# Projection-weight casts over two steps, a home for the weight of each quarter, and large roundings taken apart, in a gated cross-attention kernel

## The reference, cut to what matters

```python
ln_out = _ln(hidden_states, ln_w, ln_b)
q  = _fp8_linear_pertensor(ln_out, wq, ...)      # 16 heads; k, v: 8 groups; qx: 16 heads
core = _gqa(_ln(q), _ln(k), v)                   # self attention
xout = _gqa(_ln(qx), _ln(kx), vx)                # kx, vx = cond @ w_kv_x
cat  = concatenate([core, xout])
catq = _div_clamp_fp8(cat, proj_smooth)          # clip, then round to 8-bit floats
return einsum(catq, wproj) * (proj_in_scale * proj_w_scale)
```

## Time and profile before

| what | before |
|---|---|
| runs | 1636.44 us median of three (1634.56 to 1636.97) |
| the profiled execution, its own time | 1630.85 us |
| its span | 1629.1 us |
| TensorE busy | 1574.2 us, 97% of the span |
| VectorE busy | 1150.1 us, 71% |
| ScalarE busy | 1015.2 us, 62% |
| GpSimd busy | 486.0 us, 30% |
| DMA | 196.62 MB, 121 GB/s in the mean |
| granted TensorE clock | 0.995 in the mean |

### The profile page before, as it was taken

The page is one execution under the profiler, slowest core; times in us unless marked ns, Lnnn a source line. Parts: engine busy times, 40 slices in busy tenths (PEclk is TensorE's granted clock), DMA queues, the critical chain, the costliest instruction groups (busy, mean ns, idle before and its releaser), DMA issues.

```text
span 1629.1 us, 27708 instructions
## 1 busy us (share of the span) xinstructions
PE 1574.2 (97%) x9392; PEld 1221.4 (75%) x9392; DVE 1150.1 (71%) x2380; ACT 1015.2 (62%) x2855; POOL 486.0 (30%) x515
## 2 busy tenths in 40 slices
PE   7989979999998999999999999999999999999998
PEld 6878766666777767777777777777777777777887
DVE  6358865444997778888888887677777777898322
ACT  4354335553467877877878777777777777875100
POOL 1000222223524333443333443433443343420000
PEclk9999989999999999999999999999999999999999
DMA  8030648885663232364243353121152121110011
GB/s 304 27 109 28 229 167 271 274 270 175 215 228 124 75 135 79 101 237 143 81 136 99 106 199 116 46 77 58 46 201 66 46 109 58 46 39 7 22 38 39
DMA packets 75813, 196.62 MB, mean 121 GB/s; under 512 B 6896, under 2 KB 27376, under 8 KB 69168
## 3 DMA queue, kind: packets, MB, share of 16 engines
q1 hardware_dynamic: 70016, 176.50, 31.6%
q0 software_dynamic: 5680, 18.62, 3.9%
HBM read 147.12 MB, written 47.97 MB: 120 GB/s over the span
## 4 chain that ended last, share of the span: by engine, by line
PE 71%; DVE 8%; ACT 5%; DMA 1%; issue 1%; POOL 1%; SPq 0%; POOLq 0%; ACTq 0%; DVEq 0%
PE bank L2518 9%; PE bank L2517 9%; PE bank L99 8%; PE bank L101 8%; PE bank L100 8%; PE bank L2579 6%; PE bank L2603 5%; PE bank L2568 4%; PE bank L1423 4%; PE bank L1443 4%; PE bank L2589 3%; ACT t_sc L2734 2%; POOL t_rs L2482 1%; PE bank L1403 1%; DVE x_res L1782 1%
## 5 line engine op out<-in xcount | busy, mean ns | idle before, releaser
L2517 PE MATMUL bank<-t_half,t_xh 128*128 128x256 f16 (+1 forms) x1024 | 309.3, 326 | 0.7 <-DVE t_hn L2839 0.7
L2518 PE MATMUL bank<-t_half,t_xh 128*128 128x256 f16 (+1 forms) x1024 | 306.0, 326 | 0.0
L2479 POOL TENSOR_SCALAR t_ve<-t_ss 128x4 f32<-128x4 f32 (+1 forms) x128 | 25.6, 200 | 580.0 <-DVE t_ss L2835 554.4
L2734 ACT ACTIVATE t_sc<-bank,t_mx 128x128 f32<-128x128 f32 x512 | 180.1, 386 | 17.7 <-DVE t_mx L2875 13.1
L2839 DVE TENSOR_TENSOR t_hn<-bank,t_rs 128x256 f32<-128x256 f32 (+1 forms) x256 | 130.0, 549 | 63.4 <-POOL t_rs L2482 63.4
L2482 POOL TENSOR_TENSOR t_rs<-t_ve,t_mhalf 128x4 f32<-128x4 f32 (+1 forms) x128 | 171.0, 1336 | 10.7
L2517 PEld LDWEIGHTS bank<-t_half,t_xh 128*128 128x128 f16 x1024 | 100.3, 98 | 66.7 <-issue 1.4
L2518 PEld LDWEIGHTS bank<-t_half,t_xh 128*128 128x128 f16 x1024 | 100.2, 98 | 66.0
L2772 ACT ACTIVATE t_y<-bank,smooth 128x128 bf16<-128x128 f32 x512 | 139.3, 401 | 2.3 <-DVE t_cq L1303 2.3
L2603 PE MATMUL bank<-t_wp,t_cq 128*128 128x512 f16 x512 | 130.7, 379 | 0.0
L2579 PE MATMUL bank<-t_hT 128*128 128x128 f32 x1024 | 126.2, 276 | 2.7 <-ACT t_hT L2761 2.3
(11 more groups left out here) (355 smaller groups left out, 3878.7 us busy)
## 6 DMA issues: line engine op xcount, KB each, us to landing
t_xh<-xq_scratch SPq DMA_DIRECT2D x64, 512.0 KB, 3.5
t_cr<-in_ctxT_dram SPq DMA_DIRECT2D x64, 256.0 KB, 2.7
t_half<-w_half SPq DMA_DIRECT2D x12, 1024.0 KB, 7.6
y_rows<-s_y SPq DMA_DIRECT2D x39, 256.0 KB, 2.4
e_w<-in_w_units_dram SPq DMA_DIRECT2D x8, 1024.0 KB, 11.8
w_rows<-in_w_qkv_dram SPq DMA_DIRECT2D x8, 1024.0 KB, 5.6
xq_scratch<-z_xs SPq DMA_DIRECT2D x16, 512.0 KB, 3.3
t_slot<-w_plain SPq DMA_DIRECT2D x4, 2048.0 KB, 8.4
```

What stands on the lines that cost most here:

```text
L2517: nc.tensor.matmul(out, rows[:, k, kind, :], w[0][:, k, a:b], start=k == 0, stop=False)
L2518: last = nc.tensor.matmul(out, rows[:, k, kind, :], w[1][:, k, a:b], start=False, stop=k == KT - 1)
L2734: last = nc.scalar.activation(sc[:, h, :], b3[4 + part][:, n, :], ACT.Exp, bias=mx[:, h:h + 1], accum_out=sm[:, h:h + 1])
```

## The change

Four things are done. The projection weight gets four buffers, one for each quarter, each in the upper 8 KB of the slot that holds the quarter's q weight; one array of the dense stage (`xT_lo1`) moves to where the single buffer was, and the wait for `pj_ps` goes. The four casts of a quarter stand in two steps, 16 q + 1 and 16 q + 2, in each one before the second square of the keys and one behind the head copies. The large roundings are taken apart: in steps 4 to 7 the clamp stands behind the maxima and the two operations on the bits behind the first half of the item's rounding, in front of `normalise_b`. The slices are grouped anew over steps 1 to 6, from step 3 on with two of them in front of the second square. `LATE_FIRST` goes from 8 to 9. Cut out of the diff below are only lines that hand `m` and `quarter` on to the output product.

```diff
-LATE_FIRST = 8
+LATE_FIRST = 9
...
+    def clamp(self, dve, n):
+        y = self.y[n % 2]
+        dve.wait_ge(self.y_in, n * 4 + 4)
+        self.nc.vector.tensor_scalar(y[:].bitcast(F16), y[:], F16MAX, -F16MAX, ALU.min, ALU.max
+                                     ).then_inc(self.clamped, 1)
+
     def rounded(self, dve, c, k):
+        self.clamp(dve, c * KT + k)
+        self.rounded_bits(dve, c * KT + k)
+
+    def rounded_bits(self, dve, n):
...
+        bits = self.y[n % 2][:].bitcast(I16)
         dve.wait_ge(self.clamped, n + 1)
...
-        self.hi, self.lo = ([at(f"xT_{n}{c}", kb + 8 * i, [P, KT, CW], F32R) for c, kb in enumerate((kvx, wq, wqx, 64))]
-                            for i, n in enumerate(("hi", "lo")))
+        self.hi = [at(f"xT_hi{c}", kb, [P, KT, CW], F32R) for c, kb in enumerate((kvx, wq, wqx, 64))]
+        self.lo = [at(f"xT_lo{c}", kb, [P, KT, CW], F32R) for c, kb in enumerate((kvx + 8, 122, wqx + 8, 72))]
...
-    wp = sb("wp", 122, [P, 8, D], F16)
...
-    LAST_ROWS = (1, 3, 4, 5)
-    ROW_PIECES = {1: range(0, 3), 2: range(3, 4), 3: range(4, 6), 4: range(6, 9), 5: range(9, 12), 6: range(12, 16)}
+    wp = [sb(f"wp{q}", SLOTS[homes[q][WQ_]] + 8, [P, 8, D], F16) for q in range(Q)]
+    LAST_ROWS = (4, 5, 6, 7)
+    ROW_PIECES = {1: (0,), 2: (1, 2), 3: (3, 4, 5), 4: (6, 7, 8), 5: (9, 10, 11, 12), 6: (13, 14, 15)}
...
-            if i - 1 in LAST_ROWS:
-                sh.store(sp, (C - 1) * KT + LAST_ROWS.index(i - 1))
+            if i in LAST_ROWS:
+                sh.store(sp, (C - 1) * KT + LAST_ROWS.index(i))
...
-                last = nc.tensor.matmul(bank[5][:], cq[par][:, h, :], wp[:, h, :], start=h == 0, stop=h == KH - 1)
+                last = nc.tensor.matmul(bank[5][:], cq[par][:, h, :], wp[quarter_of(m, quarter)][:, h, :], start=h == 0,
+                                        stop=h == KH - 1)
...
         def wproj(quarter, part):
             i, a = divmod(part, 2)
-            if quarter and part == 0:
-                act.wait_ge(pj_ps, quarter * B)
             if part == 0:
                 act.wait_ge(wraw_in, quarter * 16 + 16)
...
-        def rows_part(i, part):
-            pieces = ROW_PIECES.get(number(i), ())
-            if part < len(pieces):
-                k, v = divmod(pieces[part], 4)
+        def rows_parts(i, first, last):
+            for piece in ROW_PIECES.get(number(i), ())[first:last]:
+                k, v = divmod(piece, 4)
                 sh.scaled(act, C - 1, k, (v,))
 
         def wproj_part(i, part):
-            if isinstance(i, int) and i % B == 2 and i < M:
-                wproj(i // B, part)
+            if isinstance(i, int) and i % B in (1, 2) and i < M:
+                wproj(i // B, 2 * (i % B - 1) + part)
...
                 if part:
-                    rows_part(m - 1, 0)
+                    wproj_part(m - 1, 0)
+                    rows_parts(m - 1, 0, 1 if number(m - 1) < FIRST else 2)
                 act.wait_ge(a_ps, m * 2 + part + 1)
...
             if has(i):
                 heads_out(i)
-            rows_part(i, 1)
-            wproj_part(i, 0)
+            wproj_part(i, 1)
+            if number(i) >= FIRST:
+                rows_parts(i, 2, 3)
             if has(i + 1):
                 values(i + 1, 1 - par)
-            rows_part(i, 2)
-            wproj_part(i, 1)
-            rows_part(i, 3)
-            wproj_part(i, 2)
+            rows_parts(i, 1 if number(i) < FIRST else 3, 4)
             if has(i - 1):
                 scaled_out(i - 1, quarter)
-            wproj_part(i, 3)
...
             if has(i - 1):
                 maxima(i - 1)
+                if number(i) in LAST_ROWS:
+                    sh.clamp(dve, (C - 1) * KT + LAST_ROWS.index(i))
...
             if has(i - 2):
                 rounded(i - 2, par, 0)
+            if number(i) in LAST_ROWS:
+                sh.rounded_bits(dve, (C - 1) * KT + LAST_ROWS.index(i))
...
-            if number(i) - 1 in LAST_ROWS:
-                sh.rounded(dve, C - 1, LAST_ROWS.index(i - 1))
```

More of the change, by code:

```diff
@@ L2599, in attend, with output_heads @@
                 last.then_inc(pv_ps, 1)
-        def output_heads(par, heads):
+        def output_heads(m, par, quarter, heads):
             for h in heads:
-                last = nc.tensor.matmul(bank[5][:], cq[par][:, h, :], wp[:, h, :], start=h == 0, stop=h == KH - 1)
+                last = nc.tensor.matmul(bank[5][:], cq[par][:, h, :], wp[quarter_of(m, quarter)][:, h, :], start=h == 0,
+                                        stop=h == KH - 1)
             return last
@@ L2612, in output_begin, with output_end @@
                 pe.wait_ge(x_in, m)
-            output_heads(par, range(QH))
-        def output_end(m, par):
-            output_heads(par, range(QH, KH)).then_inc(pj_ps, 1)
+            output_heads(m, par, quarter, range(QH))
+        def output_end(m, par, quarter):
+            output_heads(m, par, quarter, range(QH, KH)).then_inc(pj_ps, 1)
         def output(m, par, read, quarter):
             output_begin(m, par, read, quarter)
-            output_end(m, par)
+            output_end(m, par, quarter)
         def step(i, par, quarter):
@@ L2632, in step @@
             if has(i - 3):
-                output_end(i - 3, 1 - par)
+                output_end(i - 3, 1 - par, quarter)
             if has(i - 1):
@@ L2679, in wproj @@
             raw = slots32[homes[quarter][SPARE]]
-            last = nc.scalar.activation(wp[:, 4 * i + 2 * a:4 * i + 2 * a + 2, :], raw[:, i, 2 * a:2 * a + 2, :], ACT.Copy)
+            last = nc.scalar.activation(wp[quarter][:, 4 * i + 2 * a:4 * i + 2 * a + 2, :], raw[:, i, 2 * a:2 * a + 2, :],
+                                        ACT.Copy)
             if a:
                 last.then_inc(wp_in, 1)
-        def rows_part(i, part):
-            pieces = ROW_PIECES.get(number(i), ())
-            if part < len(pieces):
-                k, v = divmod(pieces[part], 4)
+        def rows_parts(i, first, last):
+            for piece in ROW_PIECES.get(number(i), ())[first:last]:
+                k, v = divmod(piece, 4)
                 sh.scaled(act, C - 1, k, (v,))
         def wproj_part(i, part):
-            if isinstance(i, int) and i % B == 2 and i < M:
-                wproj(i // B, part)
+            if isinstance(i, int) and i % B in (1, 2) and i < M:
+                wproj(i // B, 2 * (i % B - 1) + part)
         def squares_a(m):
```

5 lines of the change are left out of this document (removed).

## The result

The changed kernel takes 1617.31 us in the median of four executions (1614.39 to 1620.32), the kernel before 1636.7 (1634.56 to 1637.09): a ratio of 0.9884, interval 0.9864 to 0.9905. It is faster by 19 us, as forecast in sign, and by more than forecast: 1621.8 was the time, 1619.0 the lower end of the range.

The account below looks back on a forecast made before the run. TensorE's nine waits for VectorE's normalisation, 13.8 us, were taken as the recoverable loss. Savings over steps 2 to 51 summed to 14.7 us, taken as 14.6: 1636.44 - 14.6 = 1621.8 us, range 1619.0 to 1627.0.

Parts of the forecast that it names:

- the limit of 5.76 us: Latest start of VectorE's normalisation (L2839) after a step's start without cost; anything later is paid one for one.
- home per quarter: Separate projection-weight buffers remove the first cast's wait for the last old-weight product; costed at nothing, 8 us of load cover.
- late weights: LATE_FIRST 9 moves a late chunk's high parts off step 18; step 19 loses its 0.7 us more than step 35.
- The two operations beside the power: Bits operations on VectorE during GpSimd's power, steps 4 to 7: cost between 0.0 and 1.0 us per step, 0 to 0.1 taken.
- The near row: Head-stage pairing of power and two VectorE operations: at most 0.4 us longer power, 0.3 covered, 0 to 0.1 per step.
- that rival: Steps 4 to 7: bits operations start only after GpSimd's power, 4.5 us lost where 0.2 counted; 1626.1 us, chance 0.12.
- The rival of the window that is not free: ScalarE cast pushes the keys' second square; steps 3, 19, 35, 51 keep about 1 us each; 1625.8 us, chance 0.13.
- the rival of late raw weights: Casts in steps 1, 17, 33, 49 wait for 2 MB loads; 1641 us if each lands 17 us later, chance 0.02.
- the cover and the slack: 8 us between the raw weight's landing and step 1's cast, and 0.4 us by which the normalisation may be late.

Follow-up runs that it names:

- 14 stalls, two operations: Changed kernel plus two unread 128x1024 ScalarE operations in front of the output rows in 14 steps (8, 10, ..., 34): 1635.36 us, ratio 1.0001.
- three stalls put back: Changed kernel plus three unread 128x1024 ScalarE operations in front of the output rows in steps 18, 34 and 50 alone: 1628.59 us, ratio 0.9951.
- The two kernels with 14 long stalls: Changed kernel plus three or four unread ScalarE operations in front of the output rows in 14 steps: 1661.4 us with three, 1674.81 with four.

## Why the prediction was wrong in its time, point by point

**What bounds the kernel, and the limit of 5.76 us.** Right. There were nine stalls in front of one instruction, and every one that was forecast to go went, but for the 0.3 us of step 3 and the 0.2 of step 6. Step 6, with L2842 at 5.94, is 0.18 beyond the limit and 0.2 too long.

**Casts over two steps, home per quarter, late weights, roundings, slices.** Steps 35 and 51 gave 2.26 and 2.27 (2.23 forecast for each), step 19 2.89 (2.96), steps 5 and 7 1.70 and 1.96 (1.66, 1.93), step 6 1.49 (1.47), step 3 1.93 (1.80), step 2 0.43 (0.4). The sum is 14.9 us where 14.7 was worked out, and 15.0 in the stretch. The runs with one part alone bear out the parts of it, 7.1 for the casts and 4.4 for the roundings with the late chunk; the rest, 3.5, is there only together. About 2.6 of it is in steps 2 and 3, which need the slices and the rounding out of the way as well as the casts, and 0.9 in steps 5 and 7, where slices had stood in front of the output rows.

**The two operations beside the power.** The near row was the right one: 0.12 us longer power (up to 0.4 allowed), operations of 0.69 us. By the lock that the Trainium skill describes ("SBUF — State Buffer", "SBUF: two separate sides") they would, as operations in a two-port mode, have had to wait for the end of the power; in this pairing the trace does not agree (the one of 557.95 took 0.69 us inside a power that ran from 557.65 to 559.41), and that rival is out. The rival of the window that is not free is out as well (step 1's square starts on time). The raw weights were there. One price in the rival of late raw weights was reckoned wrong: with 17 us more at each of four loads, 8.6 beyond the cover and the slack, the time would be 1621.8 + 34.4 = 1656 us and not 1641; nothing else hangs on it.

**The step that failed** is the one from the profiled execution to the median: "The median of the three runs is 5.6 above the profiled one; the change touches nothing of that difference". It touches a good part of it, about 4 us by the changed kernel's own runs. Behind a stall with 1.74 us of idle time or more TensorE's clock falls to half, in some executions, and costs 1.6 us each time. The kernel before has four such stalls (steps 3, 19, 35, 51). Its profiled execution happened to have none of the falls, so its trace showed stalls at their bare price. The changed kernel has no such stall left. Of the 4.5 us by which 1621.8 missed 1617.3, 0.4 is a stretch that shrank by 15.0 instead of 14.6, and the rest is this step.

How much that is: medians give 1636.1 (74 executions of the kernel before in this study) less 1617.4 (eight of the changed one), 18.7 us; the stretch gives 15.0; 3.7 us are left, 2 to 3 falls in an ordinary execution. The intervals are wide: 15.5 to 22.3 us for the first comparison and 16.0 to 23.9 for the second, so 15.0 lies only just outside of both. The part in front of step 1 does not explain the rest, for it was not shorter in the changed kernel (505.51 and 509.45 us against 504.96, 505.76 and 506.61). All the kernels together say more. For each, this is how much less its median is than that of the kernel before on the same chip, how much less its stretch is than 905.78 with its own falls taken out, and what the median has beyond the stretch:

| kernel | median less by | stretch less by | left |
|---|---|---|---|
| changed, again | 18.7 | 15.0 | 3.7 |
| no slice in front of the output rows | 18.5 | 15.6 | 2.9 |
| casts alone | 9.9 | 7.1 | 2.7 |
| LATE_FIRST 8 again | 16.5 | 14.7 | 1.8 |
| 14 stalls, two operations | -0.9 | -2.5 | 1.7 |
| slices in their old places | 14.2 | 13.0 | 1.3 |
| roundings alone (four long stalls) | 3.9 | 4.4 | -0.5 |
| three stalls put back | 7.5 | 8.1 | -0.6 |

All six kernels without a stall of 1.74 us or more have something left, 1.3 to 3.7 us, and the two with such stalls have nothing. (The two kernels with 14 long stalls are not in the table: the number of their falls varies too much from one execution to the next.) Each median is sure to 2 to 4 us only, so it is the agreement of the rows that counts. So the loss was in the kernel before and goes with these stalls; its size is 1.3 to 3.7 us, one to three falls, and the 3.7 of the changed kernel is the upper end.

A second reckoning: the mean granted clock is 0.9924 in the 74 and 0.9954 in the eight. Among the 74 the time falls by 1.2 us for each 0.001 of clock (1639.1 in the mean at 0.990, 1633.8 at 0.994), so 0.0030 is worth 3.7 us. It is not independent, since the mean clock also holds the falls in front of the loop. That the falls are caused by the stalls is shown by the stalls put on purpose; how many there are in an ordinary execution of the kernel before is worked out from times and clocks, and no trace of it shows three of them.

The Trainium skill ("TensorE: Matmul & The Clock Gate", "Why this matters for your kernels") warns of idle gaps between bursts of matmuls. The rows agree in kind. The gap that it names is longer than any gap in the loop here, so by it no fall would have come; the measurement decides.

What the prediction wanted to see in the changed kernel's profile is all there: two waits for L2842 with 1.2 us, the steps at 15.1, the bits at 0.69. What would have warned me stood in the text: a difference of 5.6 us between one execution and the median is a third of the gain, and it was put aside without asking what it was.

## What to carry to other kernels

A stall of TensorE has two prices: its length, and half speed for a few microseconds behind it if it is long enough; here that was seen behind idle times of 1.74 us and more and not behind 1.6 us and less. 14 stalls that each add 1.25 us cost 17.9 us here and 14 that each add 2.2 us cost 44, so side work on a helper engine should be cut until no single step overruns. And when the profiled execution lies outside the timed ones, find out what it lacks (the granted clock of each execution is the first thing to compare) before its differences are carried over to the median.

## What was not expected of the hardware

- TensorE's clock fell to half behind idle stretches of 1.74 to 2.9 us, for a little over 3 us of busy work, 1.5 to 1.7 us lost each time, and not each time: 0, 1 and 2 falls in three traces of one kernel.
- Longer idle times did not bring more falls. At 1.74 to 2.2 us the one trace has 12 of 14, but the clocks of the four executions (0.981 to 0.993) say that the number varies widely; at 2.5 to 2.9 us the trace has 7 of 14, strictly every second one, and the four executions agree (0.987 to 0.988). Why is open.
- Two-operation roundings of 128x2048 keep their 0.69 us inside GpSimd's power and lengthen it by 0.12, while a context split on GpSimd had stretched one of them to 1.64.
